# The first three steps of a fused two-layer kernel: another order of the queues, late splits on GpSimd, products of ones in TensorE's first waits

## The chip, the core and the metric

The kernel runs on one core of a Trainium2 chip. The metric is the device time of one execution in microseconds (us). A core has a matrix engine (TensorE, PE in the profile), three engines for elementwise work (VectorE, DVE; ScalarE, ACT; GpSimd, POOL) and a queue that issues most transfers (SyncE, SP). Each engine works through its own instructions in the order in which they are written, and waits on semaphores that others count up.

## The reference

The input x has 128 samples of 32 channels and 512 columns; each sample has a condition vector of 128. Two layers follow, each x = x + ffn(cond(x)). Cut to what matters:

```
# layer 0
h    = gelu(c @ W0 + b0); h = gelu(h @ W1 + b1)
att  = softmax(h @ W2 + b2)                      # 8 weights per sample
u    = mix(att) @ x + att @ bias_k               # a 32x32 mixing matrix per sample
y    = u @ W_base.T + b_base
g    = 2 * softmax(log(prior + eps) + u @ router_W.T + router_b)   # over the 4 active experts
x1   = x + y + sum_e g_e * (u @ A_e.T) @ B_e.T   # rank 8 each
# layer 1
v    = conv1d(x1, 9 taps, 4 groups of 8 channels) + (c @ c_weight.T + bias)
p, i = softmax(top2(v @ gate_W.T))               # 2 of 28 experts
out  = x1 + v @ base_W.T + 2 * sum_{i} p_i * (v @ A_i.T) @ B_i.T
```

The mixing over channels and the product over columns commute, so the kernel computes x @ [A_e, router, W_base] first (it calls this u) and mixes channels afterwards. The biases and the router's constant then come in by column sums of those weights.

## The kernel before, in words

**Tiles.** 128 rows are one tile: four samples of 32 channels. There are NT = 32 tiles. Large products are made of single-rate products of rounded values: each operand is split into a high part (a cast to fp32r, by ScalarE, in rows `..._hi`) and a low part (the difference, by VectorE, `..._lo`), and a product takes three passes: hi x hi, hi x lo (`hi_passes`) and lo x hi (`lo_passes`).

**Stages of a tile.** In order: `u_half` "b" and "a", the tile times 512 + 36 columns of layer 0's weights in two PSUM banks (256 and 292 columns, four chunks of 128 rows, 12 products each); `mixing` (3 products for each half); on VectorE and ScalarE the softmax over the experts (`z0_logits`, `z0_exponent`, `g0_scaled`); `transpose_g0`, ScalarE's copy `g0t`, `low_rank_0`; VectorE's `residual` gives x1. SP stores x1 to a scratch in DRAM and loads it again as windows (`win`), three transfers. `conv` is 32 small products; VectorE transposes its result (`c1_transposed`), ScalarE and VectorE split it (`c1_high`, `c1_low`); `lows_1` gives gate logits and rank products, `base_1` the base product; VectorE's top-2 chain gives g1, `transpose_g1` and `low_rank_1` follow, then `output`.

**Steps.** Each engine's program is a function `step(s)`. Step s mixes tile s, computes u of tile s + 3 (UA), conv of tile s - 1, logits and base of tile s - 2 (LAG) and the last product of tile s - 3. Steps 0 to 2 are written out, then a loop runs steps 3 to 26 in rounds of four (UNROLL), and the rest is written out again. Steps 0 and 1 compute u of two tiles each (1 and 2, 3 and 4) since only tile 0 is done ahead of them.

**Before step 0.** The condition's small network runs on TensorE (`p_mlp`), ScalarE (gelu) and VectorE (softmax over 8). Its result att_t, 8 rows, is multiplied with `kw_sb` in eight products of 128 columns (two instructions each) into `p_mix`; VectorE and ScalarE copy the first four tiles' mixing matrices from there into `mix`. The other tiles' go by a copy `mix_raw`, and POOL spreads them from there in 16 copies, 8 in step 1 and 8 in step 2 (`mix_rest_done`); ScalarE's `mix_high` of tile 4 waits for all of them. Between these lie u of tile 0, the column sums, and on POOL the choice of the active experts' rows.

**Order.** Nothing plans the order: each queue runs as written, with `after(engine, semaphore, tile)` as a wait until that tile's count is reached. Large loads (w0 in four chunks, w1 into the same buffer, a1, b1, x and xt tiles) stand in one list on SP. ScalarE and VectorE split w1, a1 and b1 within steps 0 to 2, between the work of the tiles. TensorE ends step 2 with a wait for `b1_lo_done`.

Of the kernel before, what the change touches and what calls it, by code (L numbers as in the profile page):

```python
# [30 lines left out]
P = 128  # L31
BATCH, CH, D = 128, 32, 512
# [21 lines left out]
UA = 3  # L54
# [49 lines left out]
def build(nc, x, xt, pack, kw, rows_a, rows_b, router, active, b_base, w0, w1, a1, b1, wc, out):  # L104
# [6 lines left out]
    with ctx:  # L111
# [134 lines left out]
        batch_rows_done, lomask_0, lomask_1, lomask_2, lomask_done = sem("batch_rows_done"), sem("lomask_0"), sem("lomask_1"), sem("lomask_2"), sem("lomask_done")  # L246
# [7 lines left out]
        raw_act_done, raw_dve_done, mix_rest_done = sem("raw_act_done"), sem("raw_dve_done"), sem("mix_rest_done")  # L254
# [11 lines left out]
        eps_done = sem("eps_done")  # L266
# [48 lines left out]
        p_mlp, p_rs0, p_vrow = p_y0[:, 512:512 + P], p_y0[:, 640:640 + Z0N], p_y0[:, 680:680 + ACT0]  # L315
        p_am, p_att, p_beta0 = p_t[:, 0:MK], p_t[0:MK, P:2 * P], p_t[:, 2 * P:2 * P + NT]
        p_beta1, p_rsw0 = p_cv[:, 0:CH], p_cv
# [32 lines left out]
        def _(sp):  # L350
# [24 lines left out]
            sp.dma_start(x_sb[:, 0, :], x_v[0]).then_inc(x_loaded[0], 16)  # L375
            sp.dma_start(a1_sb[:], a1.rearrange("p (c n) -> p c n", c=HC)).then_inc(ld_a1, 16)
            load_xt(3)
            sp.wait_ge(beta1_done, 1)
            for b in range(BT):
                sp.dma_start(beta1_rows[KIM + b:KIM + b + 1], beta1[b:BATCH:BT, :]).then_inc(beta1_moved, 16)  # L380
            sp.wait_ge(ld_rows_b, 16 * ACT0)
            for n in range(1, 3):
                sp.dma_start(b0_raw[n * L0N:(n + 1) * L0N], b0_raw[0:L0N]).then_inc(copied_b, 16)
            sp.dma_start(x_sb[:, 1, :], x_v[1]).then_inc(x_loaded[1], 16)
            for n in range(2):
                sp.dma_start(wc_sb[0:KIM, n], wc.rearrange("k (g n) -> k g n", g=GROUPS)).then_inc(ld_wc, 16)
            sp.wait_ge(xt_lo_done, 1)
            load_xt(4)
            sp.wait_ge(w0_lo_done, HC)
            sp.dma_start(w_sb[:], w1.rearrange("p (c d) -> p c d", c=HC)).then_inc(ld_w1, 16)  # L390
# [30 lines left out]
        def _(pool):  # L421
# [18 lines left out]
            for n in range(0, NT, UNROLL):  # L440
                pool.memset(mix[:, n:n + UNROLL, :], 0.0).then_inc(mix_zeroed, 1)

            pool.wait_ge(ld_act, 16)
# [11 lines left out]
            pool.wait_ge(mix_zeroed, NT // UNROLL)  # L455
            pool.wait_ge(a0_done, ACT0)
            pool.wait_ge(vact_done, ACT0)
            for n in range(2):
                if n:
                    pool.wait_ge(batch_rows_done, n)  # L460
                pool.tensor_copy(win[KIM:KC, n].rearrange("k (b g) q -> k b (g q)", g=GROUPS),
# [33 lines left out]
        def _(act):  # L495
# [64 lines left out]
            def step(s):  # L560
# [15 lines left out]
                if at(s, 2):  # L576
                    z0_exponent(s)
# [668 lines left out]
```

## Time and profile before

| | us |
|---|---|
| median of 3 runs | 392.53 (391.86, 392.53, 394.56) |
| the profiled execution, its own time | 392.9 |
| its span in the profile | 391.0 |
| TensorE busy (products) | 376.3, 96% |
| VectorE busy | 272.2, 70% |
| ScalarE busy | 120.3, 31% |
| POOL busy | 40.5, 10% |
| TensorE's share of the chain that ended last | 88% |

The span is what the profiler recorded from first to last instruction; the execution's time is 1.9 us longer. TensorE's busy time counts pipelined products, so it does not say that TensorE was at its peak. In the rows, "idle before" in brackets is the time that the engine stood still ahead of the instruction, with the instruction that released it. PEclk is the granted clock of TensorE as a share of 2.4 GHz.

### The profile page before, as it was taken

The page shows a single profiled execution, that of the slowest core. Times are in us where ns is not written, and L with a number is a line of the kernel's source. Part 1 is how long each engine was busy: PE and PEld are TensorE (multiplying, and loading weights), DVE is VectorE, ACT ScalarE, POOL GpSimd, SP SyncE. Part 2 cuts the span into 40 slices and gives each one's busy share as a digit, 9 for nine tenths or more (in the row PEclk, how much of TensorE's full clock was granted, in tenths as well). Part 3 has the DMA queues.
Part 4 walks back from the last instruction along what each step waited for, and adds up shares of the span by engine and source line. Part 5 has one row for each costly group of instructions (what it writes and reads, how often), then busy time and mean ns, then how long its engine had stood idle before and what let it go on. Part 6 is the DMA issues. An engine that isn't in the chain of part 4 may idle for free.

```text
span 391.0 us, 9554 instructions
## 1 busy us (share of the span) xinstructions
PE 376.3 (96%) x3165; PEld 328.9 (84%) x3165; DVE 272.2 (70%) x940; ACT 120.3 (31%) x377; POOL 40.5 (10%) x112
## 2 busy tenths in 40 slices
PE   5998989999999999999999999999999999998986
PEld 4888968889888888889888888898888888987674
DVE  5467896678667766677677666786676666776754
ACT  6244523223322332233322322333223322222211
POOL 5727400000000000000000000000000000000000
PEclk9999989999999999999999999999999999999998
DMA  7577544776766656767766557777666566666641
GB/s 232 175 243 183 142 106 127 175 184 167 187 158 147 159 160 158 187 161 188 176 137 163 162 151 180 175 175 188 141 157 161 160 160 163 136 165 163 161 82 54
DMA packets 71019, 63.05 MB, mean 161 GB/s; under 512 B 4031, under 2 KB 53503, under 8 KB 70873
## 3 DMA queue, kind: packets, MB, share of 16 engines
q1 hardware_dynamic: 70998, 62.82, 63.8%
q8 instruction: 10, 0.16, 0.2%
q14 instruction: 9, 0.07, 0.1%
q10 hardware_dynamic: 2, 0.00, 0.0%
HBM read 45.75 MB, written 16.91 MB: 160 GB/s over the span
## 4 chain that ended last, share of the span: by engine, by line
PE 88%; DVE 6%; DMA 3%; issue 1%; ACT 1%; SPq 1%; DVEq 0%; ACTq 0%
PE p_chy L943 14%; PE p_chy L937 14%; PE p_chy L938 14%; PE p_u L937 9%; PE p_u L943 9%; PE p_u L938 8%; PE p_chy L1069 8%; PE p_t L1079 3%; PE p_y L937 2%; PE p_y L943 2%; PE p_y L938 2%; DMA win<-x_scratch 1%; DMA w_sb<-in_w 1%; PE p_y L1054 1%; DVE xt_lo L646 1%
## 5 line engine op out<-in xcount | busy, mean ns | idle before, releaser
L937 PE MATMUL p_u<-w_hi,xt_hi 128*128 128x256 f32 (+1 forms) x256 | 70.5, 302 | 2.7 <-DVE w_lo L667 2.7
L938 PE MATMUL p_u<-w_lo,xt_hi 128*128 128x256 f32 (+1 forms) x256 | 68.3, 293 | 0.0
L779 DVE STREAM_TRANSPOSE c<-p_chy 128x512 f32<-128x512 f32 x32 | 22.9, 717 | 54.3 <-PE p_chy L1069 53.9
L521 ACT CAST u_hi<-p_u 128x256 fp32r<-128x256 f32 x64 | 24.9, 389 | 106.7 <-PE p_u L943 106.7
L937 PEld LDWEIGHTS p_u<-w_hi,xt_hi 128*128 128x128 f32 x256 | 49.2, 192 | 4.0 <-issue 1.9
L938 PEld LDWEIGHTS p_u<-w_lo,xt_hi 128*128 128x128 f32 x256 | 49.4, 193 | 0.0
L937 PE MATMUL p_chy<-w_hi,c_hi 128*128 128x512 f32 x124 | 49.3, 397 | 0.0
L563 ACT CAST g1t_hi<-p_t 112x256 fp32r<-112x256 f32 x32 | 11.9, 373 | 121.3 <-PE p_t L1079 121.3
L938 PE MATMUL p_chy<-w_lo,c_hi 128*128 128x512 f32 x124 | 48.8, 394 | 0.0
L943 PE MATMUL p_u<-w_hi,xt_lo 128*128 128x256 f32 (+1 forms) x256 | 43.6, 293 | 0.6 <-DVE xt_lo L646 0.6
L943 PEld LDWEIGHTS p_u<-w_hi,xt_lo 128*128 128x128 f32 x256 | 37.0, 193 | 0.8 <-DVE xt_lo L646 0.8
L1069 PEld LDWEIGHTS p_chy<-win,wc_sb 100*32 100x32 f32 x1024 | 26.0, 109 | 12.5 <-issue 11.2
L1069 PE MATMUL p_chy<-win,wc_sb 100*32 100x128 f32 x1024 | 34.6, 276 | 1.1 <-DMA win<-x_scratch 1.1
L943 PE MATMUL p_chy<-w_hi,c_lo 128*128 128x512 f32 x124 | 33.9, 396 | 0.0
L937 PE MATMUL p_chy<-a_hi,c_hi 128*128 128x252 f32 x128 | 31.9, 283 | 0.0
L938 PE MATMUL p_chy<-a_lo,c_hi 128*128 128x252 f32 x128 | 31.7, 282 | 0.0
L674 DVE TENSOR_TENSOR u_lo<-p_u,u_hi 128x256 fp32r<-128x256 f32 x64 | 25.5, 434 | 8.4 <-ACT u_hi L521 8.3
L943 PEld LDWEIGHTS p_chy<-w_hi,c_lo 128*128 128x128 f32 x124 | 23.2, 188 | 5.4
L937 PEld LDWEIGHTS p_chy<-w_hi,c_hi 128*128 128x128 f32 x124 | 23.3, 188 | 4.5 <-issue 0.2
L938 PEld LDWEIGHTS p_chy<-w_lo,c_hi 128*128 128x128 f32 x124 | 23.4, 188 | 4.0
L937 PE MATMUL p_chy<-b_hi,g1t_hi 112*128 112x512 f32 x62 | 25.1, 405 | 1.4 <-ACT g1t_hi L563 1.4
L489 POOL COPY wc_sb<-beta_rows 4x128 f32 (+1 forms) x32 | 9.6, 299 | 159.4 <-PE p_chy L1069 159.0
(162 smaller groups left out, 747.7 us busy)
## 6 DMA issues: line engine op xcount, KB each, us to landing
win<-x_scratch SPq DMA_DIRECT2D x96, 256.0 KB, 4.3
x_scratch<-x SPq DMA_DIRECT2D x32, 260.0 KB, 2.1
xt_sb<-in_xt SPq DMA_DIRECT2D x32, 256.0 KB, 5.2
x_sb<-in_x SPq DMA_DIRECT2D x32, 256.0 KB, 5.1
out<-y_sb SPq DMA_DIRECT2D x32, 256.0 KB, 4.4
w_sb<-in_w SPq DMA_DIRECT2D x4, 256.0 KB, 4.9
w_sb<-in_w SPq DMA_DIRECT2D x1, 1024.0 KB, 5.4
a_sb<-in_a SPq DMA_DIRECT2D x1, 504.0 KB, 3.9
```

The costliest lines, as they stand in the source:

```text
L489: pool.tensor_copy(wc_sb[KIM:KC, s.mod(2)].rearrange("b g (r o) -> b g r o", r=NPH), beta1_rows[KIM:KC, s.n(), :].rearrange("b (g o) -> b ...
L521: nc.scalar.copy(u_hi[:, t.mod(4), cols], p_u[:, banks]).then_inc(u_hi_done[half], 1)
L563: nc.scalar.copy(g1t_hi[:], p_g1t).then_inc(g1t_hi_done, 1)
L646: V.tensor_tensor(xt_lo[:, t.mod(2)], xt_sb[:, t.mod(4)], xt_hi[:, t.mod(2)].bitcast(f32), ALU.subtract).then_inc(xt_lo_done, 1)
L674: V.tensor_tensor(u_lo[:, t.mod(4), cols], p_u[:, banks], u_hi[:, t.mod(4), cols].bitcast(f32), ALU.subtract).then_inc(u_lo_done[half], 1)
L779: V.transpose(c1[:], p_cv).then_inc(c1_tr, 1)
L937: mm(psum, lhs_hi, rhs_hi, start=start and n == 0, stop=False)
L938: mm(psum, lhs_hi, rhs_lo, start=False, stop=False)
L943: last = mm(psum, lhs_lo, rhs_hi, start=False, stop=stop and n == len(operands) - 1)
L1054: mm(p_y0[:, ZA + Z0N:ZB], g0t[:], b0_stack[:, 0:NY], start=False, stop=True, skip_group_check=True)
L1069: last = mm(p_cv[rows, :].rearrange("p (b g m) -> p b g m", b=BT, g=GROUPS)[:, :, g], wc_sb[:, v.mod(2), g, :], win[:, v.mod(2)].rearrange ...
L1079: last = nc.tensor.transpose(p_g1t[:, a, :], g1[:, a, :], ident[:])
```

## The change

All of it lies before step 3. Nothing is added to or taken from the loop.

- Column sums of layer 0's weights: before in 8 products of 36 columns and 8 of 512; after in 8 of 256 (`rsw0` "b", ahead of u "a" of tile 0) and 8 of 292.
- TensorE: u "b" of tile 1 ahead of step 0. The steps' order is written out anew. Step 0: mixing 0, u 1a, u 2b, transpose_g0, u 2a, low_rank_0. Step 1: u 3b, mixing 1, u 3a, u 4b, u 4a, transpose_g0. Step 2: u 5b, low_rank_0 of tile 1, conv of tile 0, u 5a, mixing 2, logits and base of tile 0, low_rank_0 of tile 2, conv of tile 1.
- beta0's small products are moved ahead of mixing's products.
- POOL: five of the eight fills of `mix` later, one of the two fills of `win` only (the other goes to VectorE, ahead of xt_hi); `z_add` of tiles 4 to 31 and `b1_lo` from VectorE to POOL.
- `mix_raw` is copied by ScalarE alone, in two halves.
- SP: w1 ahead of a1, and the small copies of `b0_raw` ahead of beta1's; wc later.
- 18 products of ones (`keep_busy`) in the condition network's and the first chunks' waits on TensorE.

The diff, cut:

```diff
+            sp.wait_ge(w0_lo_done, HC)
+            sp.dma_start(w_sb[:], w1.rearrange("p (c d) -> p c d", c=HC)).then_inc(ld_w1, 16)
             sp.dma_start(a1_sb[:], a1.rearrange("p (c n) -> p c n", c=HC)).then_inc(ld_a1, 16)
...
+            def z_rows_rest():                     # POOL
...
+                pool.tensor_tensor(z_add[:, REST], rs0[:].unsqueeze(1).to_broadcast([P, count, Z0N]),
+                                   beta0[:, REST].unsqueeze(2).to_broadcast([P, count, Z0N]), ALU.mult).then_inc(z_rest_mul, 1)
...
+                if at(s, 1):                       # POOL, end of step 1
+                    pool.wait_ge(b1_hi_done, 1)
+                    pool.wait_ge(wc_beta_done, 2)
+                    pool.tensor_tensor(b1_lo[:], b1_sb[:], b1_hi[:].bitcast(f32), ALU.subtract).then_inc(b1_lo_done, 1)
+                    pool.wait_ge(b1_lo_done, 1)
...
                 if at(s, 0):                       # ScalarE
+                    z0_exponent(s)
+                    raw_copied(0)
+                    u_high(s + 1, "a")
                     xt_high(s + 3)
+                    u_high(s + 2, "b")
+                    g0t_copied(s)
+                    raw_copied(1)
+                    u_high(s + 2, "a")
+                    xt_high(s + 4)
+                    mix_high(s + 2)
+                elif at(s, 1):
+                    u_high(s + 2, "b")
+                    z0_exponent(s)
+                    u_high(s + 2, "a")
                     act.wait_ge(ld_a1, 16)
                     nc.scalar.copy(a1_hi[:], a1_sb[:]).then_inc(a1_hi_done, 1)
+                    xt_high(s + 4)
+                    u_high(s + 3, "b")
+                    w1_high(0)
+                    u_high(s + 3, "a")
+                    g0t_copied(s)
                     mix_high(s + 2)
+                    w1_high(1)
+                elif at(s, 2):
+                    u_high(s + 3, "b")
                     act.wait_ge(ld_b1, 16)
                     nc.scalar.copy(b1_hi[:], b1_sb[:]).then_inc(b1_hi_done, 1)
+                    c1_high(s + -LAG)
+                    u_high(s + 3, "a")
+                    z0_exponent(s)
+                    xt_high(s + 4)
+                    t_exponent(s + -LAG)
+                    g0t_copied(s)
+                    act.wait_ge(mix_zeroed, NT // UNROLL)
+                    mix_high(s + 2)
...
+                if at(s, 0):                       # VectorE
                     z0_logits(s)
+                    xt_low(s + 2)
                     g0_scaled(s)
+                    u_low(s + 1, "a")
...
+                    mix_low(s + 1)
+                    u_low(s + 2, "b")
+                    xt_low(s + 3)
                     residual(s)
+                    u_low(s + 2, "a")
+                    xt_low(s + 4)
+                elif at(s, 1):
+                    z0_logits(s)
                     u_low(s + 2, "b")
+                    g0_scaled(s)
+                    u_low(s + 2, "a")
+                    mix_low(s + 1)
+                    u_low(s + 3, "b")
+                    xt_low(s + 4)
                     dve.wait_ge(a1_hi_done, 1)
                     V.tensor_tensor(a1_lo[:], a1_sb[:], a1_hi[:].bitcast(f32), ALU.subtract).then_inc(a1_lo_done, 1)
+                    u_low(s + 3, "a")
+                    w1_low(0)
+                elif at(s, 2):
+                    u_low(s + 3, "b")
+                    residual(s + -1)
+                    c1_transposed(s + -LAG)
+                    w1_low(1)
+                    c1_low(s + -LAG)
+                    z0_logits(s)
+                    u_low(s + 3, "a")
+                    g0_scaled(s)
                     mix_low(s + 1)
...
                 if at(s, 2):                       # VectorE, end of step 2
-                    dve.wait_ge(b1_hi_done, 1)
-                    V.tensor_tensor(b1_lo[:], b1_sb[:], b1_hi[:].bitcast(f32), ALU.subtract).then_inc(b1_lo_done, 1)
-                    z_rows(REST, 2)
-                    dve.wait_ge(z_add_done, 2)
+                    xt_low(s + 4)
+                    mix_low(s + 2)
+                    dve.wait_ge(z_rest_done, 1)
...
+            def keep_busy(n):                      # TensorE
+
+                for _ in range(n):
+                    mm(p_u[:, 0:P], ones_r[:], ones_r[:], start=True, stop=True)
...
             mm(p_mlp, pack_sb[:, C_W1:C_W1 + P], m1[:], start=True, stop=True).then_inc(u2_mm, 1)
+            keep_busy(4)
...
+            keep_busy(4)
             after(pe, xt_hi_done, first)
             first_chunk(0)
+            keep_busy(6)
             first_chunk(1)
+            keep_busy(4)
...
+            pe.wait_ge(beta0_done, 1)
+            column_sums(p_rsw0["b"], P, w0_hi[:, :, cols], w0_lo[:, :, cols]).then_inc(rsw0_mm, 1)
             pe.wait_ge(a0_lo_done, 1)
             u_half(first, "a")
...
-            column_sums(p_rsw0, P, w0_hi[:, :, Z0N:Z0N + D], w0_lo[:, :, Z0N:Z0N + D]).then_inc(rsw0_mm, 1)
+            _, cols = HALVES["a"]
+            column_sums(p_cv[:, 0:Z0N + NY], P, w0_hi[:, :, cols], w0_lo[:, :, cols]).then_inc(zrow_mm, 1)
+            u_half(Tile(None, 1), "b")
```

## Rows read from the trace of the kernel before

**Rows 1.** Busy time by stretch, step 3 and step 4; share columns end with PEclk, DMA share, GB/s

```profile
53.33:66.23 12.90, 12.84 (x98) 10.79 (x98) 8.92 (x31) 2.94 (x10) 0.19 (x1) 0.87 0.55 145
66.23:77.33 11.10, 11.10 (x99) 9.83 (x98) 7.96 (x29) 3.33 (x11) 0.48 (x2) 1.00 0.69 168
```

**Rows 2.** Timeline of TensorE before step 0: start us, us, engine, line, operation

```profile
17.46 0.45 PE L937 MATMUL p_u<-w_hi,xt_hi 128*128 128x292 f32 x1
17.70 0.45 PE L938 MATMUL p_u<-w_lo,xt_hi 128*128 128x292 f32 x1
...
20.55 0.26 PE L949 MATMUL p_y<-w_hi,ones_r 128*128 128x36 f32 x1
20.67 0.26 PE L950 MATMUL p_y<-w_lo,ones_r 128*128 128x36 f32 x1
...
22.19 0.39 PE L949 MATMUL p_chy<-w_hi,ones_r 128*128 128x512 f32 x1
22.42 0.40 PE L950 MATMUL p_chy<-w_lo,ones_r 128*128 128x512 f32 x1
```

**Rows 3.** Timeline of TensorE: its longer waits, mixing's products, mixing of tiles 0 and 3

```profile
8.26 0.55 PE L937 MATMUL p_u<-w_hi,xt_hi 128*128 128x256 f32 x1 [1.62 <-DVE w_lo L667]
...
10.11 0.58 PE L937 MATMUL p_u<-w_hi,xt_hi 128*128 128x256 f32 x1 [1.07 <-DVE w_lo L667]
...
11.82 3.78 PE L1003 MATMUL p_chy<-att_t,kw_sb 8*128 8x128 f32 x16
...
23.59 0.30 PE L937 MATMUL p_y<-u_hi,mix_hi 128*128 128x292 f32 x1
...
26.39 0.30 PE L1047 MATMUL p_t<-ident_r,g0s 128*101 128x128 f32 x1 [0.46 <-DVE g0s L815]
...
36.10 0.39 PE L1054 MATMUL p_y<-b_stack,g0t 101*128 101x256 f32 x1 [0.60 <-ACT g0t L599]
...
38.38 0.74 PE L943 MATMUL p_u<-w_hi,xt_lo 128*128 128x256 f32 x4 [0.56 <-DVE xt_lo L646]
...
53.33 0.40 PE L937 MATMUL p_y<-u_hi,mix_hi 128*128 128x292 f32 x1 [1.68 <-DVE b_lo L923]
...
375.53 1.08 PE L1069 MATMUL p_chy<-win,wc_sb 100*32 100x128 f32 x32 [1.10 <-DMA win<-x_scratch]
```

**Rows 4.** Granted clock of 40 slices of the span; a slice of 0.4 us

```profile
PEclk9999989999999999999999999999999999999998
...
54.80:55.20 0.40, 0.40 (x2) 0.50 0.31 63
```

**Rows 5.** Groups of VectorE's instructions from 24 to 53.4 us: count, busy us, mean ns

```profile
L687 DVE TENSOR_TENSOR w_lo<-w_sb,w_hi 128x1024 fp32r<-128x1024 f32 x2 | 2.5, 1235 | 0.0
...
L923 DVE TENSOR_TENSOR b_lo<-b_sb,b_hi 112x1024 fp32r<-112x1024 f32 x1 | 1.3, 1298 | 0.0
L693 DVE TENSOR_TENSOR z_add<-rs,beta 128x1008 f32<-128x1008 f32 x1 | 1.2, 1197 | 0.0
```

**Rows 6.** Groups of ScalarE's instructions from 24 to 53.4 us

```profile
L615 ACT CAST a_hi<-a_sb 128x1008 fp32r<-128x1008 f32 x1 | 1.0, 1040 | 0.0
```

**Rows 7.** Groups of POOL's instructions in the whole span

```profile
L480 POOL COPY mix<-mix_raw 32x224 f32<-32x224 f32 x16 | 11.9, 746 | 1.1 <-POOL g0s L471 0.2
...
L461 POOL COPY win<-ident 4x2048 f32<-4x2048 f32 x2 | 3.8, 1892 | 0.2 <-POOL vact L453 0.2
```

**Rows 8.** SP's issues for x1 of tile 0, and landing of its window loads

```profile
29.92 0.34 SPq L415 DMA_DIRECT2D x_scratch<-x  x1
32.02 1.41 SPq L401 DMA_DIRECT2D win<-x_scratch  x3
...
DMA to landing us min/median/max: 3.5/4.4/5.3
```

**Rows 9.** Timeline of VectorE before step 0: two casts of one shape

```profile
4.78 1.64 DVE L701 CAST xt_hi<-xt_sb 128x512 fp32r<-128x512 f32 x1 [2.65 <-DMA xt_sb<-in_xt]
...
6.96 0.43 DVE L662 CAST w_hi<-w_sb 128x512 fp32r<-128x512 f32 x1 [0.45 <-DMA w_sb<-in_w]
```

More of the change, by code:

```diff
@@ L588, in step, with g0t_copied @@
-                if not early and (s + 2).live():
-                    mix_high(s + 2)
-                if not early and (s + 4).live():
-                    xt_high(s + 4)
-                t = s + (s.c + 1 if early else UA)
-                if t.live():
-                    u_high(t, "b")
-                if at(s, 1) or at(s, 2):
-                    u_high(t, "a")
-                if s.live():
-                    after(act, g0_tr, s)
+                def g0t_copied(v):
+                    after(act, g0_tr, v)
@@ L608, in step, with w1_high, raw_copied @@
-                if t.live() and not at(s, 1) and not at(s, 2):
-                    u_high(t, "a")
+                def w1_high(n):
+                    half = slice(n * HC // 2, (n + 1) * HC // 2)
+                    act.wait_ge(ld_w1, 16)
+                    nc.scalar.copy(w1_hi[:, half], w_sb[:, half]).then_inc(w1_hi_done, 1)
+                def raw_copied(n):
+                    half = slice(n * RAW, (n + 1) * RAW)
+                    nc.scalar.copy(mix_raw[:, half], p_mix[:, half]).then_inc(raw_act_done, 1)
@@ L877, in step @@
                     V.tensor_copy(logits[:], p_h1[:, L1N:H1N]).then_inc(logits_done, 1)
-                    if not early and (s + 2).live():
+                    if not at(s, 2) and (s + 2).live():
                         mix_low(s + 2, lambda: after(dve, logits_done, v))
@@ L915, in step @@
                     g0_scaled(s + 1)
-                if not early and (s + UA).live():
+                if not early and not at(s, 2) and (s + UA).live():
                     u_low(s + UA, "b")
@@ L1001, in _ @@
             pe.wait_ge(att_t_done, 1)
+            for b in range(BT):
+                last = mm(p_beta0[by_batch[b]], kw_sb[:, CH * CH:CH * CH + CH],
+                          att_t[:].rearrange("k (t b) -> k b t", b=BT)[:, b, :], start=True, stop=True)
+            last.then_inc(beta0_mm, 1)
             for m in range(CH // BT):
@@ L1151, in step @@
                     low_rank_1(s + -LAG)
+                elif at(s, 0):
+                    mixing(s)
+                    u_half(s + 1, "a")
+                    u_half(s + 2, "b")
+                    transpose_g0(s)
+                    u_half(s + 2, "a")
+                    low_rank_0(s)
+                elif at(s, 1):
+                    u_half(s + 2, "b")
+                    mixing(s)
+                    u_half(s + 2, "a")
+                    u_half(s + 3, "b")
+                    u_half(s + 3, "a")
+                    transpose_g0(s)
+                elif at(s, 2):
+                    u_half(s + 3, "b")
+                    low_rank_0(s + -1)
+                    conv(s + -2)
+                    u_half(s + 3, "a")
+                    mixing(s)
+                    lows_1(s + -LAG)
+                    base_1(s + -LAG, lambda: transpose_g0(s))
+                    low_rank_0(s)
+                    conv(s + -1)
+                    transpose_g1(s + -LAG)
                 else:
```

254 lines of the change are left out of this document (113 added, 141 removed).

## The prediction

> **What bounds the kernel now.** I first read the table of engines and the slices: TensorE is busy in 96% of the span, and the chain that ended last is 88% TensorE. I then cut the span by steps [rows 1]. A steady step takes 11.10 us with TensorE busy in all of it, and nothing in the diff touches a steady step, the drain at the end, or the amount of work. So the change can only move the moment at which step 3 starts (53.33 before) and what step 3 itself costs. Step 3 takes 12.90 us, 1.8 more than step 4, at a mean granted clock of 0.87: 12.90 x 0.13 = 1.7 us are the clock's. Then I read TensorE's timeline up to 55 us for its waits [rows 3], the clock in short windows behind the longest of them [rows 4], and the queues of the other engines for what those waits stand behind [rows 5 to 9].
>
> Two things are to be seen in the timeline. **The start is slow**: in tile 0's products 292 columns take 0.24 us, which is the 1.2 GHz level, and later 512 columns take 0.23 us, the 2.4 GHz level [rows 2]. The granted clock shows 1.00 there, so the spacing has to be read; the rise lies between 18 and 22. **The start has holes**: TensorE idles for 0.46, 0.60 and 0.56 us in steps 0 and 1, and for 1.68 us ahead of step 3's mixing, which waits for VectorE's b_lo and z_add [rows 3]. 1.5 us after that last hole the clock is at 0.50 [rows 4].
>
> **The sum, on the profiled execution (392.9 us, span 391.0; it lies 0.4 above the median of the three runs, and I leave that difference alone).**
>
> *Column sums.* Before: 8 products of 36 columns, 0.11 apart, and 8 of 512, 0.23 apart: 2.75 us [rows 2]. After: 8 of 256 and 8 of 292 columns at 0.46 ns a column: 2.0 us. **-0.75 us.** Both versions spend the same moments at the low level; which products fall into them doesn't matter.
>
> *TensorE's order, from mixing of tile 0 to mixing of tile 3.* Before this stretch is 53.33 - 23.59 = 29.74 us [rows 3]. Its work at 0.46 ns a column: five u tiles 15.0, three mixings 2.25, two convs 2.0 (from the start at 375.53 to the next row's, they are 1.0 each), logits and base of tile 0 1.4 + 2.8, low rank and transposes 1.1; 24.6 in all. So 5.1 us are lost: 3.3 as idle time, the rest as drain and restart around each hole. The new order has the same work (half a u tile, 1.4 us, is done ahead of it). I went through the new queues, each instruction at its row's duration, started at the latest of its waits. Steps 0 and 1 come out without a hole: u of the next tile always lies between a tile's mixing and the transposition of its g0, two halves of it (3.0 us) or more where one half (1.4) and a hole of 0.46 lay before [rows 3], so the chain of z0, exp, alpha and g0 is covered, and ScalarE's copy of it too. What is late next is in step 2:
> - logits of tile 0 wait for c_hi and c_lo: w_lo (1.24) now stands between the transposition of c and c_lo on VectorE [rows 5]: 0.5 us.
> - low_rank_0 of tile 2 waits for g0t, which stands behind t_exp on ScalarE, which waits for top-k on VectorE: 0.4 us.
> - conv of tile 1 waits for its windows. The residual of tile 1 is moved from step 1 to step 2, behind a_lo (as long as w_lo), w_lo (1.24) and two u_lo on VectorE, and these behind a_hi and w_hi (1.04 and about the same) on ScalarE [rows 5, 6]. I get x1 at 40.7. The store starts 2.1 us ahead of the window loads, and the last of these lands 5.3 us after its issue [rows 8], so the windows are there at 48.2; TensorE comes at 47.3: 0.9 us.
> - restarts, 0.15 each, and slack for what my hand working misses in steps 0 and 1: 0.8 us.
>
> Together 2.6 us where 5.1 were. Ends: 1.4 (all but the windows hidden) and 4.0 (x1 1.4 us later). **-2.5 us.**
>
> *Splits on POOL.* b_lo (1.30) and z_add (1.20 for its first half) leave VectorE [rows 5]; that takes away the 1.68 us hole, counted above. On POOL the trace has no two-input operation of this size. Lower end: its copy of 2048 elements in 1.89 us, so 1.0 us for 1024; upper end: its copy of 224 in 0.75 us, so 3.4 us [rows 7]. I take 1.9, two streams at the rate of the long copy, which is the nearest row in shape. Behind b_lo on POOL stand g0's last columns of tile 2, eight mix copies (6.0 us) and wc; behind those copies ScalarE's mix_hi of tile 4, and behind that g1t_hi. b_hi is ready at about 40, POOL is through at 48.5, g1t_hi is wanted at 50: 1.5 us of cover, none left at the upper end. **0.** That VectorE loses nothing beside it is my choice; one pair of rows speaks against it: a cast of 128x512 took 1.64 us while POOL filled mix with zeros, and one of the same shape 0.43 after that [rows 9]. The Trainium skill, GPSIMD Engine Reference, section 1 (Specifications), says the same as a rule: GpSimd's SBUF interfaces are shared with VectorE, with contention for VectorE's instructions that have two SBUF inputs, and its section 3 gives a two-input operation there 1.96 times VectorE's time, 2.5 us for b_lo (an estimate). By that rule w_lo, which runs beside b_lo ahead of c_lo, would come up to 1.2 us later, and the sum would be 389.2; no row shows the two together.
>
> *Moved off the path, at nothing.* ident_r, iota_e and one window fill on VectorE lie ahead of xt_hi, where VectorE idles 2.65 us [rows 9]; without that cover they cost up to 2.3 us, POOL's 1.89 for the fill and two small copies [rows 7]. Loading w1 (1 MB) ahead of a1 and xt of tile 3: those two are wanted at 26 us or later. beta0's small products ahead of mixing's: moved, 0.3 us each way. SP issues the same transfers.
>
> *Products of ones.* 18 products of 128 columns, 0.11 each at the low level, 1.9 us in all. They lie in the holes that end at 8.26 and 10.11 (1.62 and 1.07) and beside ScalarE's second gelu [rows 3]; 0.0, and 0.1 each if a hole is shorter. Whether they lift the clock earlier no row shows. Between 11.8 and 15.5 TensorE was busy throughout with mixing's products of 8 rows, and the clock did not rise until five us of 128-row products had followed; so I take the same moment for the rise. **0.**
>
> *The clock in step 3.* The fall followed a hole of 1.68 us; a hole of 1.10 us near the end (375.53) was not followed by one before the last product [rows 3]. My largest new hole is 0.9, with one of 0.4 ahead of it. So it does not fall: **-1.7 us.**
>
> 392.9 - 0.75 - 2.5 - 1.7 = **388.0 us**.
>
> **Rivals.**
> - *The clock falls again.* If x1 of tile 1 comes 0.8 us later than I have it, the hole ahead of conv is as long as the old one, and it falls close behind the other. For it: mine is a hand working over some forty instructions. 388.0 + 1.7 = 389.7, up to 391.1 with the waits at 4.0.
> - *The products of ones lift the clock before mixing's products.* These 16 instructions take 3.78 us at the low level [rows 3], half of it at the high one: 388.0 - 1.9 = 386.1. Against it: the holes are filled only up to 11.6. The Trainium skill, TensorE: Matmul & The Clock Gate, Part 1, says that the default state is throttled and activity releases the throttle, which is this rival's rule; the trace agrees for 20 us, and cannot say whether these products suffice.
> - *The waits only change place.* TensorE loses 5.1 us in the new order too, and the clock falls: 392.9 - 0.75 = 392.1. For it: VectorE's lateness made three of the four holes, and its work hardly shrinks before 50 us.
> - *POOL becomes the bound, slower than before.* If b_lo costs 7 us (twice the upper end, for two streams) and the eight copies stretch by half beside VectorE (as VectorE's cast did by more than that [rows 9]), POOL is through 8.1 us later, 6.6 beyond its cover, and ScalarE's queue stands: 388.0 + 6.6 = 394.6. It loses to before once POOL ends later than 54.9.
>
> **How the numbers follow.** Forecast 0.52, clock falls again 0.27, early clock 0.08, waits change place 0.08, POOL 0.05. Range 386.0 to 391.3: from the early clock to the clock's fall with the waits at 4.0; it leaves out the last two rivals and a tail. 1% of 392.5, about what a measurement tells from no change, is 3.9 us: faster means below 388.6. The forecast's own spread (386.8 with waits at 1.4, 389.4 at 4.0) gives three quarters of its 0.52, the early clock all, the clock's fall a sixth: 0.51. Slower by over 1% is part of the POOL rival, 0.03. The rest, 0.46, is within 1%.
>
> **What would show each step.** Step 3's mixing should start at 50.1 (53.33 before) and step 3 last 11.1. Products of 8 rows should still be 0.24 us each. The longest wait of TensorE after 12 us should be conv on win in step 2, below 1.3 us; if it is over 1.6, look for a granted clock of 0.50 behind it. Holes in steps 0 or 1 would make my hand working wrong; a wait of ScalarE's mix_hi on POOL past 50 would bring in the last rival.

## The result and the profile after

The kernel after takes 389.76 us (median of 5 runs, 389.53 to 389.93) against 393.01 for the one before (5 runs, 391.86 to 394.56) on the same chip: a ratio of 0.9917, 95% interval 0.9894 to 0.9940. Measured again later, on the chip that also ran seven of the kernels below, it takes 389.63 (10 runs) against 392.49, 0.9909 (0.9880 to 0.9939). In the ratios of this document slow executions are left out: one of 601.4 us at a granted clock of 0.57 (of the kernel with b_lo earlier), and two of 397 to 398 us among the 19, and two among the 21, of before. The profiled execution takes 389.76 us with a span of 388.0 (before 392.9 and 391.0). So 3 us are gained, 0.8%, which the interval tells from nothing; the forecast had 4.9.

First the two stretches of the kernel after that answer to [rows 1], step 3 and step 4 (the columns are the same; the clock and the DMA share stand behind the engines):

```profile
52.09:63.26 11.17, 11.17 (x98) 9.78 (x98) 8.53 (x31) 3.27 (x11) 0.19 (x1) 1.00 0.70 190
63.26:74.36 11.10, 11.10 (x99) 9.82 (x98) 7.88 (x29) 3.33 (x11) 0.48 (x2) 1.00 0.69 168
```

Step 3 starts 1.24 us earlier and is 1.73 us shorter, with the clock at 1.00 in it; 1.24 + 1.73 is the whole 3.0 of the span. From step 4's mixing on the two kernels take 324.8 and 324.7 us. Then TensorE's timeline, which answers to [rows 3]: mixing's products, mixing of tile 0, every wait between 12 and 53 us, and the one near the end:

```profile
12.44 3.78 PE L1077 MATMUL p_chy<-att_t,kw_sb 8*128 8x128 f32 x16
...
24.67 0.30 PE L996 MATMUL p_y<-u_hi,mix_hi 128*128 128x292 f32 x1
...
36.10 0.37 PE L996 MATMUL p_u<-w_hi,xt_hi 128*128 128x292 f32 x1 [0.27 <-DVE u_lo L736]
...
45.15 0.74 PE L1002 MATMUL p_chy<-a_hi,c_lo 128*128 128x252 f32 x4 [0.77 <-DVE c_lo L840]
48.19 0.31 PE L1118 MATMUL p_t<-ident_r,g0s 128*101 128x128 f32 x1 [0.44 <-DVE g0s L871]
51.49 0.43 PE L1153 MATMUL p_t<-ident,g 128*112 128x128 f32 x2 [0.50 <-DVE g L965]
52.09 0.40 PE L996 MATMUL p_y<-u_hi,mix_hi 128*128 128x292 f32 x1 [0.16 <-DVE x L827]
...
372.50 1.08 PE L1141 MATMUL p_chy<-win,wc_sb 100*32 100x128 f32 x32 [1.08 <-DMA win<-x_scratch]
```

Steps 0 and 1 hold one wait of 0.27 where three of about half a us stood in [rows 3], and the 1.68 is gone. But in step 2 stand three waits for VectorE that the forecast had at 0.5, 0 and 0, and the wait for the windows, which it had as the longest, is not there. VectorE and POOL in that stretch show why. VectorE first:

```profile
39.04 1.22 DVE L749 TENSOR_TENSOR w_lo<-w_sb,w_hi 128x1024 fp32r<-128x1024 f32 x1
...
41.11 0.71 DVE L835 STREAM_TRANSPOSE c<-p_chy 128x512 f32<-128x512 f32 x1
41.74 2.75 DVE L749 TENSOR_TENSOR w_lo<-w_sb,w_hi 128x1024 fp32r<-128x1024 f32 x1
44.41 0.68 DVE L840 TENSOR_TENSOR c_lo<-c,c_hi 128x512 fp32r<-128x512 f32 x1
...
46.32 0.55 DVE L864 TENSOR_TENSOR g<-z,alpha 128x32 f32<-128x32 f32 x1
46.90 0.62 DVE L868 CAST g0s<-g 128x64 fp32r<-128x64 f32 x1
47.55 0.58 DVE L871 TENSOR_TENSOR g0s<-g,g0s 128x32 fp32r<-128x32 f32 x1
```

And POOL beside it:

```profile
41.00 2.40 POOL L513 TENSOR_TENSOR b_lo<-b_sb,b_hi 112x1024 fp32r<-112x1024 f32 x1 [5.05 <-ACT b_hi L655]
43.47 1.07 POOL L488 CAST g0s<-beta 128x5 fp32r<-128x5 f32 x1
44.60 5.47 POOL L496 COPY mix<-mix_raw 32x224 f32<-32x224 f32 x8
```

The second w_lo, the same instruction as the first on the other half, takes 2.75 us instead of 1.22. It starts at 41.74; b_lo ends on POOL at 43.40, 1.66 later; what is left of w_lo after that is 1.09. It looks as if w_lo had stood still until POOL was through. The scalings of g0, 0.19 to 0.20 when nothing runs beside them, take 0.55 to 0.62 beside POOL's copies of 0.65 to 0.7: three of these copies end at 46.81, 47.46 and 48.08, and the scalings at 46.87, 47.52 and 48.13. Two short instructions of the top-2 chain end in the same way behind the last two copies (0.41 and 0.55 for 0.17 and 0.23), and g, which TensorE waits for 0.50, stands behind them. Not every VectorE instruction is held. The transposition of c, whose source is in PSUM, keeps its 0.71 in the middle of b_lo, and a reduction and MAX8, with one small operand in SBUF, keep their 0.16 and 0.19 inside POOL's copies. That is the theory that the experiments test.

### The profile page after: what moved, and what is told of

It reads as the page before. It is cut to its first block, busy times and chain, and to the rows that moved or that the text cites. A ratio compares the mean times of both kernels' runs of the same rounds, so it can differ in the third digit from the quotient of the medians.

```text
span 388.0 us, 9591 instructions
## 1 busy us (share of the span) xinstructions
PE 376.9 (97%) x3183; PEld 331.3 (85%) x3183; DVE 276.4 (71%) x937; ACT 121.1 (31%) x379; POOL 41.7 (11%) x114
## 4 chain that ended last, share of the span: by engine, by line
PE 89%; DVE 5%; DMA 3%; issue 1%; ACT 1%; SPq 1%; DVEq 0%; ACTq 0%
PE p_chy L996 14%; PE p_chy L1002 14%; PE p_chy L997 14%; PE p_u L996 9%; PE p_u L997 8%; PE p_u L1002 8%; PE p_chy L1141 8%; PE p_t L1153 3%; PE p_y L996 2%; PE p_y L1002 2%; PE p_y L997 2%; DMA win<-x_scratch 1%; DMA w_sb<-in_w 1%; PE p_y L1125 1%; PE p_chy L1077 1%
```

## The experiments

**Theory 1:** while a POOL instruction reads and writes SBUF, certain VectorE instructions (some of those with all operands in SBUF) stand still until its end, and this turned the forecast's small waits in step 2 into 1.7 us. **Theory 2:** the order of VectorE's queue is simply too long, whoever runs beside it. **Theory 3:** the gain has to do with the removal of b_lo and z_add from VectorE alone, or with the products of ones. Every run stands against runs of before on the same chip; each expectation stood before its run.

### b_lo on POOL earlier

```diff
 # ScalarE, end of step 1 and start of step 2
-                    w1_high(1)
+                    act.wait_ge(ld_b1, 16)
+                    nc.scalar.copy(b1_hi[:], b1_sb[:]).then_inc(b1_hi_done, 1)
                 elif at(s, 2):
                     u_high(s + 3, "b")
-                    act.wait_ge(ld_b1, 16)
-                    nc.scalar.copy(b1_hi[:], b1_sb[:]).then_inc(b1_hi_done, 1)
+                    w1_high(1)
```

> The changed kernel with b_hi ahead of w_hi's second half on ScalarE, so POOL's b_lo starts at about 39.9 instead of 41.0. Theory 1 (VectorE stands still until POOL's running instruction ends, whenever it needs the port that they share): w_lo's second half starts at 41.7, b_lo ends at 42.3 instead of 43.4, so w_lo takes 1.7 us instead of 2.75, TensorE's wait for c_lo (0.77) goes, and step 3 starts about 1.0 earlier: 388.8. Theory 2 (the order alone made VectorE late, POOL's share is small): w_lo's time falls by less than 0.3 and the kernel takes 389.5 to 389.8.

Measured: 388.54 us (median of seven runs, 388.09 to 390.62; the eighth is the 601.4), ratio 0.9905 (0.9876 to 0.9934). VectorE's and then POOL's row:

```profile
41.65 1.88 DVE L749 TENSOR_TENSOR w_lo<-w_sb,w_hi 128x1024 fp32r<-128x1024 f32 x1
```

```profile
39.70 2.75 POOL L513 TENSOR_TENSOR b_lo<-b_sb,b_hi 112x1024 fp32r<-112x1024 f32 x1 [3.83 <-ACT b_hi L652]
```

b_lo now ends at 42.45, 0.80 behind w_lo's start, and w_lo takes 0.80 + 1.08. It also works the other way: b_lo started while the first w_lo (38.96 to 40.18) was running, and took 2.75 instead of 2.40. The wait for c_lo is gone, step 3 starts at 51.13 (52.09 in the kernel after), and the wait for the windows appears, 0.63. On the same chip the kernel after takes 389.63, 1.1 more. The ratios to the runs of before beside each (0.9905 and 0.9909) do not tell the two kernels apart; the starts of step 3 and the rows do.

### b_lo in four pieces

```diff
-                    pool.tensor_tensor(b1_lo[:], b1_sb[:], b1_hi[:].bitcast(f32), ALU.subtract).then_inc(b1_lo_done, 1)
+                    for n in range(4):
+                        part = slice(n * D // 4, (n + 1) * D // 4)
+                        pool.tensor_tensor(b1_lo[:, :, part], b1_sb[:, :, part], b1_hi[:, :, part].bitcast(f32), ALU.subtract).then_inc(b1_lo_done, 1)
```

> The changed kernel with b_lo in four pieces on POOL, 0.6 to 0.7 us each. Theory 1 (VectorE stands still only until the running POOL instruction ends): w_lo's second half waits for one piece, then runs, 1.2 to 1.9 us instead of 2.75; the time falls by 0.5 to 0.9, to 389.1. Rival (the two share a bandwidth in proportion): w_lo takes 2.75 as before, and the time stays at 389.8.

Measured: 389.48 (4 runs), ratio 0.9921 (0.9890 to 0.9952). VectorE's rows:

```profile
41.98 1.19 DVE L751 TENSOR_TENSOR w_lo<-w_sb,w_hi 128x1024 fp32r<-128x1024 f32 x1
43.08 1.24 DVE L842 TENSOR_TENSOR c_lo<-c,c_hi 128x512 fp32r<-128x512 f32 x1
```

The first piece ends at 42.00, just as w_lo starts, and w_lo takes its normal 1.19; POOL pays, with 4.36 us for the four pieces (41.26 to 45.62), and c_lo, 0.68 when free, waits once for a piece. Step 3 started at 50.97, as early as in the swap. But the time did not follow, and TensorE's waits say where it went:

```profile
49.43 1.08 PE L1143 MATMUL p_chy<-win,wc_sb 100*32 100x128 f32 x32 [0.98 <-DMA win<-x_scratch]
62.02 1.08 PE L1143 MATMUL p_chy<-win,wc_sb 100*32 100x128 f32 x32 [0.71 <-DMA win<-x_scratch]
```

The windows of tile 2 were issued only at 55.04 (53.42 in the swap of b_hi and w_hi above, whose store was as early), and step 3 took 12.24 us instead of 11.1, at a granted clock of 1.00. SP waited 3.3 us for the store of x1 to land, 1.5 in the swap. Why the store took so long no run separates.

### b_lo and z_add back on VectorE

```diff
-                if at(s, 0):                       # POOL
-                    z_rows_rest()
...
-                    pool.tensor_tensor(b1_lo[:], b1_sb[:], b1_hi[:].bitcast(f32), ALU.subtract).then_inc(b1_lo_done, 1)
...
-                    dve.wait_ge(z_rest_done, 1)    # VectorE, end of step 2
+                    dve.wait_ge(b1_hi_done, 1)
+                    V.tensor_tensor(b1_lo[:], b1_sb[:], b1_hi[:].bitcast(f32), ALU.subtract).then_inc(b1_lo_done, 1)
+                    z_rows(REST, 2)
+                    dve.wait_ge(z_add_done, 2)
```

> The changed kernel with b_lo and z_add of tiles 4 to 31 back on VectorE at the end of step 2. Theory 1: w_lo's second half is back at 1.2 us and c_lo is 1.5 earlier, but b_lo (1.3) then stands between xt_lo and step 3's mixing, so the start of step 3 is at about 52.2 as it is now, and the clock does not fall: 389.8, between 389.3 and 390.5. Rival (the moves to POOL are what closed the hole): the hole of 1.7 us is back and the clock falls behind it, 391.5 to 393.

Measured: 392.19 (10 runs, 389.84 to 393.24), ratio 0.9995 (0.9974 to 1.0015). TensorE's waits at the end of step 2, and then step 3 as a stretch:

```profile
48.81 1.08 PE L1137 MATMUL p_chy<-win,wc_sb 100*32 100x128 f32 x32 [1.11 <-DMA win<-x_scratch]
51.85 0.61 PE L992 MATMUL p_y<-u_hi,mix_hi 128*128 128x292 f32 x1 [1.59 <-DVE b_lo L978]
```

```profile
51.85:65.54 13.69, 13.69 (x97) 12.10 (x98) 8.91 (x31) 2.93 (x10) 0.85 (x2) 0.79 0.53 136
```

My theory's time (389.8) missed, and the rival came: the hole for b_lo is back, and the mean clock of step 3 is 0.79. The new order starts step 3 at 51.85, but in this profile mixing of tile 0 had started 0.74 earlier than in the kernel after (23.93); the stretch between them takes 27.92, 0.5 more. The one run of ten in which the granted clock stayed at 1.0 took 389.84. So the splits on POOL are worth 2.4 to 2.6 us in this order, most of it through the clock. What theory 1 says of VectorE did come: with b_lo off POOL the second half of w_lo takes 1.36 for the 2.75, beside POOL's copies.

### No products of ones

```diff
             def keep_busy(n):
-                for _ in range(n):
+                for _ in range(0):
```

> The changed kernel without its 18 products of ones. Theory 1 (they do not lift the clock, and the third group stands in front of att's transposition, which starts at 11.30 though att is ready at 10.5): mixing's products start 0.5 earlier, 12.0, the moment of the clock's rise is where it was, and the time falls by 0.2 to 0.4: 389.5. Rival (they keep the clock's rise early): the rise to the 2.4 GHz level comes 1 us or more later, and the time is 390.3 or more.

Measured: 389.63 (4 runs), ratio 0.9926 (0.9897 to 0.9955), the kernel after's own time to 0.13. Without the ones mixing's products start at 12.23 and still take 3.78 us, and products of 292 columns are 0.24 apart up to 20.79, as they are up to 20.76 with them. What they do, if anything, is smaller than the spread of the runs (389.13 to 389.98).

### The hole of before filled

```diff
 # kernel before, TensorE, end of step 2, ahead of the wait for b1_lo_done
+                    for _ in range(28):
+                        mm(p_h1[:, 0:P], ones_r[:], ones_r[:], start=True, stop=True)
```

> The kernel before with 28 products of ones (128 columns) in the hole at the end of step 2, nothing else. They fill 1.5 of its 1.7 us. Theory (the granted clock falls because TensorE idled there): no fall, step 3 takes 11.1 to 11.2 instead of 12.9, start of step 3 unchanged at 53.3, time 1.7 lower than before: 391.2. Rival (the fall has another cause): step 3 still 12.9, 392.9.

Measured: 392.55 (10 runs) against 392.68 for before (19 runs), ratio 0.9997 (0.9953 to 1.0041). The products lie in the hole, and step 3 behind it is a step at full clock:

```profile
50.49 3.32 PE L1182 MATMUL p_chy<-ones_r 128*128 128x128 f32 x28
```

```profile
53.65:64.70 11.05, 11.05 (x99) 9.77 (x99) 7.88 (x29) 2.94 (x10) 0.19 (x1) 1.00 0.65 167
```

Against [rows 1] that is the same step with 1.85 us less: in this profile it is the hole, not anything in step 3's work, that brings the clock's fall. The time of this kernel settles nothing, for two reasons. The interval of the ratio is wider than the effect. And the fill was too long: the 28 products lie 0.11 apart and hold TensorE for 3.16 us, not for the 1.5 that I had written. b_lo ends at 51.97, and in the kernel before mixing follows 0.44 behind it, so mixing would have come at about 52.4; it came at 53.65, and 1.2 of the 1.85 us were spent on the products. One profile does not say how often the clock is kept.

### Only the moves to POOL, in the old order

```diff
 # kernel before
+                if at(s, 0):                       # POOL
+                    z_rows_rest()
...
+                if at(s, 2):
+                    pool.wait_ge(b1_hi_done, 1)
+                    pool.wait_ge(wc_beta_done, 3)
+                    pool.tensor_tensor(b1_lo[:], b1_sb[:], b1_hi[:].bitcast(f32), ALU.subtract).then_inc(b1_lo_done, 1)
+                    pool.wait_ge(b1_lo_done, 1)
```

> The kernel before with one part of the change alone: z_add of tiles 4 to 31 on POOL in step 0, b_lo on POOL at the end of step 2, where VectorE has only short instructions. b_hi is ready at 49.6, b_lo takes 2.4 us on POOL, so mixing of tile 3 starts at about 52.2 instead of 53.3, the hole is 0.7 instead of 1.7, and the clock does not fall: 392.9 - 1.1 - 1.7 = 390.1. Rival (VectorE's short instructions beside b_lo each wait for its end, theory 1 taken to small operations): g1 and x1 of tile 2 come up to 2 us later, the hole stays 1.5 or more, and the clock falls: 392.5 to 393.5.

Measured: 394.5 (10 runs, 392.85 to 396.38), ratio 1.0011 (0.9966 to 1.0056). VectorE, POOL and TensorE at the end of step 2:

```profile
51.01 2.31 DVE L923 TENSOR_TENSOR gate<-gate_a,gate_b 128x28 f32<-128x28 f32 x1
53.36 0.39 DVE L926 TENSOR_TENSOR g<-p_chy,gate 128x224 f32<-128x224 f32 x1
```

```profile
50.92 2.36 POOL L511 TENSOR_TENSOR b_lo<-b_sb,b_hi 112x1024 fp32r<-112x1024 f32 x1 [6.65 <-ACT b_hi L650]
```

```profile
53.81 0.43 PE L1097 MATMUL p_t<-ident,g 128*112 128x128 f32 x2 [1.26 <-DVE g L926]
55.11 0.40 PE L955 MATMUL p_y<-u_hi,mix_hi 128*128 128x292 f32 x1 [0.87 <-DVE x L792]
```

My theory's time (390.1) missed, and what the rival says of VectorE came. This is the clearest row of the study: an instruction on 28 columns, 0.19 us elsewhere, takes 2.31 because it began 0.09 behind b_lo, and ends when b_lo ends (53.28). Moving an instruction of 1.3 us off VectorE cost VectorE 2.1. In the profile, which is of the fastest of the ten runs (392.85), step 3's mixing starts at 55.11, 1.8 later than before; in step 0 TensorE waits 2.12 for g0s, which stands behind an xt_lo of 2.21 us (0.68 when free) beside z_add on POOL. The clock did not fall behind waits of 1.26 and 0.87. Neither the order alone (the experiment with b_lo and z_add back on VectorE) nor these moves alone gains; they need each other.

### ScalarE spreads the second half of the mix copies

To b_lo's earlier place this kernel adds:

```diff
 # POOL
-                    if at(s, 1) or at(s, 2):
+                    if at(s, 1):
...
 # ScalarE, step 2
+                    raw_spread(2)                  # four copies
                     z0_exponent(s)
                     xt_high(s + 4)
+                    raw_spread(3)                  # four copies
                     t_exponent(s + -LAG)
```

> The kernel after, with ScalarE's cast b_hi ahead of the second half of w1_high (as the earlier swap), and with the eight mix copies of step 2 on ScalarE instead of POOL. Theory (a VectorE instruction stands still while a POOL instruction runs): g0's scalings of step 2, 0.55 to 0.62 us each beside those copies, fall back to 0.2; TensorE's wait for g0s in step 2 (0.5 in the swap) goes, step 3's mixing starts at about 50.6 (51.13 in the swap), with the wait ahead of conv of tile 1 grown to about 1.0: 388.3 to 388.6. Rival (the cost lies in the order of VectorE's queue, not in POOL's copies): the scalings stay at 0.5 to 0.6, and ScalarE, with eight more copies, delays z_exp and t_exp: 388.8 or more.

Measured: 388.90 (6 runs, 387.18 to 390.90), ratio 0.9888 (0.9837 to 0.9938). VectorE's rows for g0 and TensorE's waits:

```profile
46.64 0.19 DVE L873 TENSOR_TENSOR g<-z,alpha 128x32 f32<-128x32 f32 x1
46.87 0.20 DVE L877 CAST g0s<-g 128x64 fp32r<-128x64 f32 x1
47.10 0.19 DVE L880 TENSOR_TENSOR g0s<-g,g0s 128x32 fp32r<-128x32 f32 x1
```

```profile
47.34 0.31 PE L1127 MATMUL p_t<-ident_r,g0s 128*101 128x128 f32 x1 [0.58 <-DVE g0s L880]
49.72 0.39 PE L1134 MATMUL p_y<-b_stack,g0t 101*128 101x256 f32 x1 [1.10 <-ACT g0t L610]
```

Theory 1's row came: without POOL's copies each scaling takes 0.2. The rival's wait came too: a copy takes ScalarE 0.62 us (four in 2.50), not the 0.3 that I had assumed when I wrote the queue, so z_exp and t_exp come late. In this profile the clock was at 0.50 from about 51.8 and step 3 took 12.61 at a mean of 0.87. Two of the six runs took 390.9, one of them this one; the others 387.2 to 389.4.

### The same with quarters, and with x1 earlier

The second kernel adds b_lo in four pieces and drops the third group of ones; the third also moves VectorE's residual:

```diff
-                    w1_low(0)                      # end of step 1
                 elif at(s, 2):
-                    u_low(s + 3, "b")
                     residual(s + -1)
+                    u_low(s + 3, "b")
+                    w1_low(0)
```

> As c1, and b_lo on POOL in four pieces, and the third group of four products of ones taken out. Theory: the second half of w_lo takes 1.2 us again, c_lo is in time, mixing's products start at 12.0 to 12.2; what is late next is conv of tile 1 on its windows, 1.0 us or more: step 3's mixing at about 50.3, 388.0. Rival: the windows' and stores' place in SP's queue decides, as in the run with b_lo in quarters, where step 3's conv waited for windows twice for 1.7 us in all: 389.3.

> As c2, with VectorE's residual of tile 1 ahead of the first half of the low part of w1 and of u_low 5b in step 2. Theory (the wait of conv for its windows is set by x1 of tile 1): x1 comes 0.7 or more earlier, the wait shrinks by as much, step 3's mixing starts at about 49.8 and the time is 0.4 below c2's. Rival (the windows land late because of the DMA queues, not of x1): no change against c2, within 0.2, or u's pass over the low part waits instead.

Measured: 388.93 (6 runs, 388.15 to 391.77), ratio 0.9898 (0.9847 to 0.9949), and 389.51 (12 runs), ratio 0.9931 (0.9910 to 0.9952). Both keep the 1.1 us for g0t, since ScalarE's order is the same. In the second kernel mixing's products start at 11.82 and step 3 at 50.90, and the clock fell behind the wait. The second half of w_lo took 1.60 there, not the 1.2 of the expectation: it started 0.52 before the third piece's end, and 1.08 were left behind it. No wait for the windows came, so the third kernel had none to shrink. In it x1 is stored 0.95 earlier (39.49 for 40.44), but the first half of w_lo now runs beside b_lo and takes 1.60, and TensorE waits for c_hi 0.18 and c_lo 0.41 (0.33 for c_lo in the second): nearer to the rival, and no gain.

> The kernel after, unchanged, beside the other three: 389.8 as before, every theory alike. It gives what c1 to c3 are compared with on the same chip; a difference of 0.3 us to the first measurement is the spread between chips.

The kernel after, again: 389.63, as in the first measurement (389.76). The two profiles start step 3 at 51.85 and 52.09.

### ScalarE's copies in its gaps

```diff
                     w1_high(1)
+                    raw_spread(0, 1)               # copy numbers
                     c1_high(s + -LAG)
                     u_high(s + 3, "a")
-                    raw_spread(2)
+                    raw_spread(1, 3)
                     z0_exponent(s)
                     xt_high(s + 4)
-                    raw_spread(3)
+                    raw_spread(3, 6)
                     t_exponent(s + -LAG)
                     g0t_copied(s)
+                    raw_spread(6, 8)
                     mix_high(s + 2)
```

> As c1 (ScalarE spreads the eight mix copies of step 2, b_hi ahead of the second half of w1_high), with those copies one to three at a time into the stretches in which ScalarE stood still in the swap (one ahead of c_hi, two ahead of z_exp, three ahead of t_exp, two behind g0t) and without the third group of products of ones. They took 0.62 us each in c1, where t_exp came at 49.13 and TensorE waited 0.58 for g0s and 1.10 for g0t. Theory (POOL's copies held VectorE, and in c1 ScalarE's order spent the gain): g0's scalings at 0.2, t_exp at about 47.5, no wait for g0t; conv of tile 1 waits 0.5 to 1.0 for its windows; step 3's mixing starts at about 50.3, no fall of the clock: 387.9. Rival (ScalarE's late mix_hi of tile 4, or its copies behind g0t, hold g1t_hi): a new wait of about 1 us and 388.8.

> As c4, with residual of tile 1 ahead of the first half of the low part of w1 and u_low 5b behind both, and b_lo on POOL in four pieces. Theory (x1 sets conv's wait): x1 of tile 1 comes 0.7 us earlier, conv's wait on its windows shrinks by that, step 3's mixing at about 49.9, 387.5. Rival (as in c3: the half of w_lo that is moved beside b_lo is held, and c_lo comes late by what x1 gains): as c4 or up to 0.6 more.

Measured on one chip: the first 387.59 (6 runs, 386.87 to 388.75), ratio 0.9863 (0.9819 to 0.9906), the fastest kernel of the study, 1.4% below before. The second 388.15 (6 runs), ratio 0.9882 (0.9839 to 0.9926). TensorE in the first:

```profile
48.90 1.08 PE L1151 MATMUL p_chy<-win,wc_sb 100*32 100x128 f32 x32 [0.86 <-DMA win<-x_scratch]
49.92 0.43 PE L1163 MATMUL p_t<-ident,g 128*112 128x128 f32 x2
50.10 0.38 PE L1007 MATMUL p_y<-u_hi,mix_hi 128*128 128x292 f32 x1
...
60.45 1.08 PE L1151 MATMUL p_chy<-win,wc_sb 100*32 100x128 f32 x32 [0.39 <-DMA win<-x_scratch]
```

With POOL out of step 2 but for b_lo, and ScalarE's queue in order, the two waits left between mixing of tile 0 and of tile 3 are 0.27 for u_lo and 0.86 for the windows. The second half of w_lo still takes 1.87 beside b_lo, but c_lo is in time. In the second kernel the windows are in time, but c_lo is late by 0.71 beside the pieces of b_lo: x1 earlier and b_lo beside w_lo cancel, as in the run before.

**What they tell apart.** Theory 1 holds for the large differences, the scalings and the gate: with b_lo earlier, in pieces, or beside another instruction, VectorE waits as long as POOL's running instruction still needs. Theory 2 falls with the first kernel of the last section (ScalarE's copies in its gaps), in which VectorE has the same queue as in the kernel after and is late for nothing but the 0.27. From mixing of tile 0 to mixing of tile 3 the kernel after takes 27.42, with b_lo earlier 26.56, and with the eight copies on ScalarE too 25.83. Of theory 3 the ones fall, and the removal from VectorE alone, in the old order, gains nothing.

## Why the prediction was right or wrong

The time, 389.76, lies inside the range of 386.0 to 391.3, 1.8 above the forecast of 388.0, and the gain of 0.8% is within the 1%. Of the three terms of the sum the clock's came, the column sums' came nearly, and that of TensorE's order did not.

**Column sums, -0.75: right in size, and mostly eaten by a late start.** Rows of after that answer to [rows 2]:

```profile
17.59 0.41 PE L1008 MATMUL p_t<-w_hi,ones_r 128*128 128x256 f32 x1
17.81 0.41 PE L1009 MATMUL p_t<-w_lo,ones_r 128*128 128x256 f32 x1
...
22.58 0.30 PE L1009 MATMUL p_chy<-w_lo,ones_r 128*128 128x292 f32 x1
22.72 0.29 PE L1008 MATMUL p_chy<-w_hi,ones_r 128*128 128x292 f32 x1
```

The 256-column sums lie before the clock's rise (0.21 apart), but as I had assumed u's products take their place behind it. From mixing's products to mixing of tile 0 before took 23.59 - 11.82 = 11.77 us; after 24.67 - 12.44 = 12.23, with half a u tile (1.42) more in it and beta0's small products (0.26) less: 11.07, 0.7 gained. Ahead of that it started 0.62 later, 0.26 of them beta0's products and 0.36 lateness. The products of ones were costed at nothing; the run without them starts mixing's products 0.21 earlier, but the kernel after starts at 11.63 in its second profile and 12.44 in the first, so this lateness is no firm figure. Net -0.34 (24.67 - 1.42 - 23.59).

**TensorE's order, -2.5: the step that failed; it gave -0.9.** From mixing of tile 0 to mixing of tile 3 before lost 5.1 us over its work. After takes 27.42 for 23.2 of work: 4.2 lost where I had 2.6. Of these, 2.1 are waits (0.27, 0.77, 0.44, 0.50 and 0.16) where I had 1.8, and 2.1 are drain and restart around them and gaps too short for the list, where "restarts, 0.15 each, and slack" had 0.8: around the wait of 0.77 alone the products lie 1.05 further apart than their columns ask for. Steps 0 and 1 came out as worked, with one wait of 0.27 against the 0.8 of slack. In step 2 "logits of tile 0 wait for c_hi and c_lo" was 0.77, not 0.5; "low_rank_0 of tile 2 waits for g0t" did not come, a wait of 0.44 for g0s did; the wait for the windows did not come since TensorE was late anyway; and g of the top-2 chain and x were late by 0.50 and 0.16. The forecast costed every VectorE instruction at a duration without POOL beside it, and each wait that this makes brings a restart with it.

That is the sentence "that VectorE loses nothing beside it is my choice", under **Splits on POOL, 0**. b_lo itself was near its price (2.40 for 1.9) and POOL was through with its copies at 50.07; ScalarE's mix_hi of tile 4 waited for that until 50.15, which cost nothing, since g1t_hi was not due before 51.5. What was wrong was to hold back one pair of rows [rows 9] against many without such a pair. The kernel with ScalarE's copies in its gaps measures what the choice cost: with POOL's copies gone from step 2 and b_lo earlier, the same stretch takes 50.10 - 24.27 = 25.83, so 2.6 are lost, with 0.86 for the windows. Step 3 starts at 50.1, and that profiled execution takes 388.14, beside the forecast's 2.6, 0.9, 50.1 and 388.0. So where POOL seldom holds VectorE the sum of this term comes out. Its parts do not: 1.1 are waits and 1.5 the rest, where the forecast had 1.8 and 0.8, and neither of its waits for c and g0t came. This kernel also has another ScalarE order and four ones fewer, step 3 took 11.54 in it, and the agreement to a tenth is luck.

The Trainium skill, GPSIMD Engine Reference, section 1, was cited as the rule that speaks against the choice, with 389.2 by it; 389.76 was measured. It names VectorE's instructions with two SBUF inputs, which fits w_lo and the gate. The Trainium skill, SBUF — State Buffer, "Who interferes with whom", is more exact than what I cited: whichever of the two starts first has the shared ports for its whole instruction, and the other is blocked entirely. The trace agrees in both directions: 0.80 + 1.08 for w_lo, 1.66 + 1.09 for it in the kernel after, 2.75 for b_lo behind the first w_lo. Casts and copies with one SBUF input were held too (g0s 0.62); the same page covers this where they run in its two-port mode, and no run here shows which mode they ran in. My 1.2 us, a mere excess in proportion, was 1.53 here, and would be the rest of b_lo in any order.

**The clock, -1.7: right.** Step 3 is 1.73 shorter. The longest wait between 12 us and step 3 was 0.77, and none of the kernels with waits of up to 0.98 in the profile shows a fall behind them. The rival that the clock falls was the right one to keep: it came behind a hole of 1.59 with one of 1.11 three us ahead, and, in two profiles of three, behind a wait of 1.10 with one of 0.3 to 0.6 ahead of it. Waits of 1.26 and then 0.87, and one of 2.12 in step 0 of the same kernel, did not bring it. So the length of the longest hole alone does not decide, and I can't say what does.

**Moved off the path and products of ones, 0: right** within 0.2 for the ones, though their price was read wrong: at the low level they lie 0.21 apart, not 0.11, and 18 of them fill 3.9 us, not 1.9. Most of that lay in waits. **The other rivals:** the early clock did not come with mixing's products at the high level. In some profiles the clock rises once early, in the kernel after as well as without ones, and mixing's products take 3.78 us in all of them. POOL did not become the bound; with the moves alone the kernel is no faster than before, for the reason of theory 1.

**The sum.** Forecast -0.75 - 2.5 - 1.7 = -4.9; measured on the profiled executions -0.3 - 0.9 - 1.7 = -3.0 of the span. The missing 2.0 are 1.6 in TensorE's order, where VectorE was held and the restarts were priced too low, and 0.4 of the late start. The time came out at 389.8, which is also the number of the rival "the clock falls again" (389.7), by quite another way: whoever had read only the time would have believed the wrong cause.

## What to carry to other kernels

Costing a move to POOL at "hidden" needs a second look: not at POOL's own slack, but at which SBUF-to-SBUF instruction of VectorE starts while it runs. That one lasts until POOL's ends, so a long POOL instruction belongs where VectorE works from PSUM or waits, or cut in pieces. And where a chain of short VectorE instructions decides when TensorE goes on, copies of 0.7 us on POOL cost more than on ScalarE, if they lie in ScalarE's gaps. When several small changes only pay together (here the order and the moves: nothing that can be told from noise each, 3 us together), test each alone before it is called useless.

## What the runs showed that I had not expected

- A VectorE instruction of 0.19 us took 2.31 beside one POOL instruction, and POOL's b_lo, 2.36 to 2.40 with little beside it, took 2.75 behind a VectorE instruction and 4.36 in four pieces; transpositions and additions from PSUM kept their durations (0.71 and 0.68).
- Behind a run of short fills the wait does not end with the running one. In the kernel after, a cast that takes 0.18 in the kernel before takes 1.67: it starts beside POOL's fills of `mix`, which are 0.46 each and follow one another at once, and ends at 3.86, when the third of them has ended (3.83). Cutting work into pieces let VectorE in between b_lo's pieces, but not between these fills:

```profile
2.19 1.67 DVE L701 CAST iota_e<-iota_e_i 128x28 f32<-128x28 int32 x1
```

```profile
2.38 1.45 POOL L445 MEMSET mix<- 128x512 f32 x3
```

- A copy of 32x224 takes ScalarE 0.62 us and POOL 0.70: the small shape costs nearly the same on both.
- The granted clock can rise to the high level early, fall, and rise again, without an effect on the time. The second profile of the kernel after shows it in the slices, and in products of ones 0.11 apart (four in 0.64) where they were 0.21 in the first (four in 1.09):

```profile
PEclk9589999999999999999999999999999999999999
```

```profile
6.07 0.64 PE L1037 MATMUL p_u<-ones_r 128*128 128x128 f32 x4
...
11.63 3.78 PE L1077 MATMUL p_chy<-att_t,kw_sb 8*128 8x128 f32 x16
```
